# Four chained layers on eight images: fewer projections in layer 1, symmetric halves in layer 3, folded norms, and GpSimd shares

## The chip, the cores and the metric

The kernel runs on one core of a Trainium2 chip. The metric is the time of one execution on the device in microseconds (us). The core has five engines that work side by side, each through its own queue in program order: TensorE (PE; the weight loads of its matmuls are shown apart as PEld), VectorE (DVE), ScalarE (ACT), GpSimd (POOL) and SyncE (SP), which here only issues DMAs. They meet through semaphores alone.

## The reference

The input is eight images of 16 x 16 positions with 128 channels, all fp32. Four layers follow each other:

```
L0: theta, phi, g = x@w_theta, maxpool2x2(x@w_phi), maxpool2x2(x@w_g)   (with biases)
    x1 = x + sigma * (softmax(theta phi^T) g @ w_o + b_o)                256 positions against 64 pooled ones
L1: n = groupnorm(x1; 32 groups) * gamma + beta;  q, k, v = n@wq+bq, n@wk+bk, n@wv+bv
    x2 = x1 + softmax(q k^T / sqrt(128)) v @ wo + bo                     one head of 128
L2: n = groupnorm(x2; 16 groups) * scale + bias;  q, k, v = n@w_qkv
    x3 = x2 + concat_8_heads(softmax(q k^T / 4) v) @ w_out + b_out       eight heads of 16
L3: z = DHT2d(x3)  (cas transform over channels and over w);  zn[h,w] = z[-h,-w]
    o1k = relu(.5(z w1a + zn w1b) + b1_0),  o1n = relu(.5(zn w1a + z w1b) + b1_1)   (8 blocks of 16 channels)
    y = (two block matmuls of o1k, o1n);  out = x3 + DHT2d(softshrink(y, 0.01)) / (16*128)
```

The position reversed in h and w is the same image read backwards, modulo 16 in both directions.

## The kernel before

Everything is unrolled and everything stays in SBUF after the first loads. A layout with channels on the partitions (128 x 256) and one with positions on the partitions (two tiles of 128 positions x 128 channels) alternate. PSUM is used as eight banks of 512 fp32; each matmul group is given its bank by hand (the `b` argument) and waits, where the order of the queue doesn't ensure it, for the semaphore that frees the bank (the `*marks`, through `freed`).

One image passes through these steps. Layer 0: `proj0`, `pool0` (max pooling), `theta`, `pg_out`, `s0` (scores), `nmax0_out`, `exp0`, `p0t` (transposition of the probabilities), `p0c`, `gwm`/`gw` (the values), `o0` (with a column of ones that gives the sums), `inv0_out`, `x1_out` (positions on partitions, divides by the sums and adds `xin`, the input loaded a second time in that layout). Then `x1t`/`xc` transpose to channels on partitions, and the group norm follows: `moments`, `mean`, `mean_square` on DVE, `gm1` on PE (mean over the group), `variance`, `variance_eps`, `inverse_deviation` on POOL (a power of -0.5), `group_scale`, `group_shift`, `normalised`. Layer 1: `qk1` (two projections), `q1`, `k1`, `v1m`/`v1`, `s1`, `nmax1_out`, `exp1`, `p1t`, `p1c`, `o1`, `inv1_out`, `x2_out`; `x1b_out` and `x2b_out` on POOL add the bias of the layer to the residual. `x2t`/`xc` and the same norm lead to layer 2: `qk2`, `qkE`/`qkO`, `v2m`/`va`, `sm` (scores for the maximum, heads in two sets g = 0, 1, four heads at a time in row groups of the array), `nmax2_out`, `nt`, `nc_out`, `spread` (a DMA that writes the negated maxima as a row beside q), `st` (scores transposed, with the maximum in them), `exp2`, `pv`, `oc`, `ot`, `oinv_out`, `on_out`, `ont`, `onc`, `o2`, `x3_out`. Layer 3: `zm`, `zc`, `wrap` (POOL copies row 0 to row 16, so that the reversed read is a plain negative stride), `am` (two accumulated matmuls over 17 x 17 = 289 columns, the second reading `zE` backwards), `o1k_out`, `o1n_out`, `ym`, `yh`, `yn`, `v3`, `s3_out`, `om`, `xo`, `store`.

The eight images are interleaved by an order that is written out for each queue (L319 to L325 for POOL, L630 to L681 for PE, L816 to L837 for ACT, L1021 to L1061 for DVE, L264 to L266 for SP). `keep_clock(n, b)` puts n matmuls on zeros into the PE queue; nobody reads them. The first `sm` in PE's order is that of image 0 (L641); after the last `pv`, that of image 7 (L679), only the ends of images 5 to 7 are left.

The input comes in by `load_x` and `load_tokens` for each image (128 KB each) and four tables of weights.

```python
both = bank[b][:, 0:EXT].rearrange("p (h w) -> p h w", h=HE)
mm(both, fold1[:, 0, :], zE(i), start=True, stop=False)
mm(both, fold1[:, 1, :], zE(i)[:, ::-1, ::-1], start=False, stop=True).then_inc(s["a"], 1)
```

Of the kernel before, what the change touches and what calls it, by code (L numbers as in the profile page):

```python
# [23 lines left out]
EXT = HE * WE  # L24
# [5 lines left out]
COLUMNS = ("b_phi_g", "b_theta", "sigma", "L1_conv_gn_gamma", "L1_conv_gn_beta", "L1_conv_bq", "L1_conv_bk",  # L30
# [15 lines left out]
def table(t):  # L46
# [23 lines left out]
    at("cas_w")[:] = np.kron(np.eye(tile_h), cas(W))  # L70
# [43 lines left out]
def build(nc, x, xT, weights, out):  # L114

    x_tok = x.rearrange("b (u h) w c -> b (h w) u c", u=TILES)
    out_tok = out.rearrange("b (u h) w c -> b (h w) u c", u=TILES)

    with ExitStack() as ctx:
# [14 lines left out]
        def col(name):  # L134
# [5 lines left out]
        wvo, bo1_wide = sb("wvo", [P, C]), sb("bo1_wide", [P, C])  # L140
        w2qs = sb("w2qs", [P, C])
# [7 lines left out]
        bq_s, c_t0, c_t1, c_low, c_high, half = (  # L149
            sb(n, [P, 1]) for n in ("bq_s", "c_t0", "c_t1", "c_low", "c_high", "half"))  # L150
# [4 lines left out]
        xin = ring("xin", [P, TILES, C], IMAGES)  # L155
# [62 lines left out]
        def wide(tile):  # L218
            return tile.unsqueeze(1).to_broadcast((P, TILES, C))
# [5 lines left out]
        def _(sp):  # L225
            def load_x(i):
                sp.dma_start(x0T(i), xT[i]).then_inc(s[f"x0T{i}"], 16)

            def load_tokens(i):
                sp.dma_start(xin(i), x_tok[i]).then_inc(s[f"xin{i}"], 16)  # L230
# [34 lines left out]
            spread(3, 1); store(1); spread(4, 0); spread(4, 1); spread(5, 0); store(2); spread(6, 0); spread(5, 1)
            spread(6, 1); spread(7, 0); store(3); spread(7, 1); store(4); store(5); store(6); store(7)  # L266
# [3 lines left out]
        def _(pool):  # L270
            gp = nc.gpsimd

            def fill():
# [39 lines left out]
            def wrap(i):  # L313
# [763 lines left out]
```

## Time and profile before

| what | value |
| --- | --- |
| runs of the kernel before | 174.29, 173.12, 173.66 us; median 173.66 us |
| profiled execution: time | 173.37 us |
| profiled execution: span from the first to the last instruction | 171.5 us |
| PE busy in the span | 96% |
| granted clock of TensorE, mean over the span | 0.999 |

The profiled execution took 1.9 us outside its span. A busy PE is not a PE at its peak: matmuls are pipelined, and one that is shown with 400 ns may be followed by the next after half of that. What a matmul costs is the distance from start to start, which the chain of work shows.

### The profile page before, as it was taken

The numbers are of one execution on the slowest core, as the hardware profiler recorded it, in microseconds if no ns is written. First come the engines' busy times: TensorE is split into PE (matmuls) and PEld (weight loads), VectorE is DVE, ScalarE is ACT, GpSimd is POOL, SyncE is SP. The second block draws the span as 40 slices with busy tenths as digits, with TensorE's granted clock in tenths as the row PEclk, the third lists the DMA queues.
The fourth block names the chain that finished last, engine by engine and source line by source line (L and its number), as shares of the span: only waits on it lengthen the run. The fifth ranks groups of instructions, "written<-read, shape, count | busy, mean of one in ns | idle before, by whom it ended". The sixth has DMA issues, their size and how long they took to land.

```text
span 171.5 us, 3846 instructions
## 1 busy us (share of the span) xinstructions
PE 164.8 (96%) x1473; PEld 124.0 (72%) x1473; DVE 109.1 (64%) x293; ACT 109.4 (64%) x251; POOL 27.5 (16%) x56
## 2 busy tenths in 40 slices
PE   7999979999999999999999999999999999999992
PEld 4687869887767777686888776677857675657881
DVE  1368899899977886837967634979175566123032
ACT  0467568686565788385467877374867856874660
POOL 8011714232122111120011210000011000000100
PEclk9999999999999999999999999999999999999999
DMA  5992000000000000000001001000010000200003
GB/s 139 303 325 108 4 2 2 0 4 0 2 2 4 0 4 6 0 6 0 0 4 34 2 0 36 0 6 2 2 36 2 4 2 2 64 3 6 0 0 92
DMA packets 6353, 5.17 MB, mean 30 GB/s; under 512 B 576, under 2 KB 5952, under 8 KB 6336
## 3 DMA queue, kind: packets, MB, share of 16 engines
q1 hardware_dynamic: 6336, 4.93, 9.5%
q8 instruction: 12, 0.20, 0.4%
q14 instruction: 5, 0.04, 0.1%
HBM read 3.75 MB, written 1.05 MB: 28 GB/s over the span
## 4 chain that ended last, share of the span: by engine, by line
PE 83%; DMA 4%; DVE 4%; ACT 3%; SPq 2%; issue 1%; POOL 0%; DVEq 0%; POOLq 0%
PE psum L537 10%; PE psum L517 9%; PE psum L548 9%; PE psum L445 4%; PE psum L465 4%; DMA x0T<-in_xT 3%; PE psum L599 3%; PE psum L425 2%; PE psum L559 2%; PE psum L455 2%; ACT pT L779 2%; PE psum L618 2%; PE psum L600 2%; PE psum L610 2%; PE psum L575 2%; PE psum L589 2%
## 5 line engine op out<-in xcount | busy, mean ns | idle before, releaser
L984 DVE TENSOR_REDUCE nmax<-psum 128x4 f32<-128x1024 f32 x32 | 38.1, 1216 | 9.1 <-PE psum L517 8.9
L779 ACT ACTIVATE pT<-psum 128x1024 f32<-128x1024 f32 x32 | 32.1, 1022 | 9.3 <-PE psum L537 9.3
L537 PE MATMUL psum<-qk 17*128 17x256 f32 (+1 forms) x256 | 18.3, 400 | 0.2 <-DMA qk<-stage_all 0.2
L517 PE MATMUL psum<-qk 16*128 16x256 f32 (+1 forms) x256 | 18.3, 400 | 0.0
L548 PE MATMUL psum<-pT,vaug_all 128*32 128x256 f32 x256 | 16.5, 384 | 0.0
L517 PEld LDWEIGHTS psum<-qk 16*128 16x128 f32 (+1 forms) x256 | 11.6, 184 | 4.9 <-issue 1.8
L537 PEld LDWEIGHTS psum<-qk 17*128 17x128 f32 (+1 forms) x256 | 11.6, 184 | 4.1 <-ACT oT L784 0.8
L311 POOL TENSOR_TENSOR rstd<-vare,half 128x1 f32<-128x1 f32 x16 | 8.9, 564 | 31.9 <-DVE vare L936 31.8
L548 PEld LDWEIGHTS psum<-pT,vaug_all 128*32 128x32 f32 x256 | 7.1, 109 | 6.0 <-issue 2.3
L316 POOL COPY zE<-zE 128x17 f32<-128x17 f32 x8 | 1.6, 200 | 52.6 <-ACT zE L792 52.6
L784 ACT COPY oT<-psum 128x256 f32<-128x256 f32 x16 | 6.0, 373 | 5.9 <-PE psum L548 5.8
L304 POOL TENSOR_TENSOR x2b<-x,tab 128x256 f32<-128x256 f32 x8 | 5.8, 727 | 24.5 <-DVE x L974 24.5
L298 POOL TENSOR_TENSOR x1b<-x,bo_wide 128x256 f32<-128x256 f32 x8 | 5.8, 730 | 22.4 <-DVE x L906 22.4
L339 PE MATMUL psum<-busy 128*128 128x256 bf16 x43 | 8.2, 338 | 1.1 <-POOL busy L274 1.1
L1011 DVE SCALAR_TENSOR_TENSOR yneg<-psum,c_high,yhigh 128x256 f32<-128x256 f32 x8 | 3.8, 479 | 7.8 <-ACT yhigh L810 7.8
L990 DVE RECIPROCAL oinv<-psum 128x16 f32<-128x16 f32 x8 | 2.0, 254 | 10.4 <-PE psum L559 10.4
L465 PE MATMUL psum<-v_all,p1T 128*128 128x129 f32 x64 | 8.6, 277 | 0.0
L445 PE MATMUL psum<-k1T,q1T 128*128 128x256 f32 x32 | 8.6, 393 | 0.0
L742 ACT ACTIVATE p<-psum,nmax 128x256 f32<-128x256 f32 x16 | 6.7, 469 | 2.9 <-DVE nmax L962 2.7
L465 PEld LDWEIGHTS psum<-v_all,p1T 128*128 128x128 f32 x64 | 7.9, 191 | 0.7 <-issue 0.5
L752 ACT COPY xT_sb<-psum 128x256 f32<-128x256 f32 x16 | 6.0, 373 | 2.7 <-PE psum L474 1.5
L1018 DVE TENSOR_TENSOR x<-psum,x 128x256 f32<-128x256 f32 x8 | 3.4, 423 | 6.6 <-PE psum L626 6.5
(137 smaller groups left out, 360.1 us busy)
## 6 DMA issues: line engine op xcount, KB each, us to landing
x0T<-in_xT SPq DMA_DIRECT2D x8, 128.0 KB, 4.9
xin<-in_x SPq DMA_DIRECT2D x8, 128.0 KB, 5.0
out<-x SPq DMA_DIRECT2D x8, 128.0 KB, 2.0
tab<-in_weights SPq DMA_DIRECT2D x1, 580.0 KB, 5.3
qk<-stage_all SPq DMA_DIRECT2D x32, 4.0 KB
tab<-in_weights SPq DMA_DIRECT2D x1, 448.0 KB, 5.4
tab<-in_weights SPq DMA_DIRECT2D x1, 384.0 KB, 5.7
tab<-in_weights SPq DMA_DIRECT2D x1, 200.0 KB, 2.5
```

Source lines behind the costliest of these rows:

```text
L311: gp.tensor_tensor(rstd[k](i), vare[k](i), half[:, :], ALU.pow).then_inc(s[f"rstd{layer}"], 1)
L339: mm(bank[b][:, 0:256], busy[:, 0:P], busy[:, :], start=True, stop=True)
L445: last = mm(bank[b][:, u * TOK:(u + 1) * TOK], q1T(i)[:, u * P:(u + 1) * P], k1T(i), start=True, stop=True)
L465: last = mm(bank[b][:, u * (C + 1):(u + 1) * (C + 1)], p1T(i)[:, m, u * P:(u + 1) * P], v1_all[:, i % SLOTS, m, :], start=(m == 0), stop=( ...
L517: last = mm(bank[(b0, b1)[j // 2] + j % 2][:, u * TOK:(u + 1) * TOK], at[:, u, 0, :], at[:, :, 1, :], start=True, stop=True)
L537: last = mm(bank[(b0, b1)[j // 2] + j % 2][:, m * TOK:(m + 1) * TOK], at[:, m, 1, :], at[:, :, 0, :], start=True, stop=True)
L548: last = mm(bank[b][32 * j:32 * j + 32, 0:TOK], vaug_all[:, i % SLOTS, m, QUADS * g + j, :], pT[g](i)[:, j, m, :], start=(m == 0), stop=(m ...
L742: last = go(p1(i)[:, u, :], bank[home["s1", i]][:, u * TOK:(u + 1) * TOK], ACT.Exp, bias=nmax1(i)[:, u:u + 1])
L752: copy(xT_sb[layer - 1](i), bank[home[f"x{layer}t", i]][:, 0:TOK]).then_inc(s[f"xT{layer}"], 1)
L779: go(pT[g](i)[:, 2 * k:2 * k + 2].rearrange("p j m t -> p j (m t)"), pair(home["st", g, i][k]), ACT.Exp).then_inc(s["exp" + "EO"[g]], 1)
L784: copy(oT[g](i), bank[home["pv", g, i]][:, 0:TOK]).then_inc(s["oT" + "EO"[g]], 1)
L984: v.tensor_reduce(nmax2[g](i)[:, :, 2 * k:2 * k + 2], pair(home["sm", g, i][k]).rearrange("p j (u m) -> p u j m", u=TILES), AX.X, ALU.max, ...
```

## The change

Layer 1. The score matrix (n wq + bq)(n wk + bk)^T is written as n (wq wk^T) n^T plus a term for each key position; terms that are the same for all keys of a query fall out of the softmax, but the exponential's bias has to carry the rest. `qk1` is now one projection with a product of weights made once (`w1qk`), `k1` is gone, `s1` takes the normalised image itself as the other operand. A further column of `v1m` gives `e1`, and `score_shift` (POOL) makes the bias `nb1` of `exp1` from it and `nmax1`. The gammas and betas of both norms are folded into weights and bias columns at the start (`fold_biases`, `bias_wide`, `fold_values`, `fold_biases2`, `fold_out2`, `scaled2`, `values_folded`, `bias_sums`, `bias_sums2`, `out2_folded`); `group_scale` and `group_shift` go, and `normalised` subtracts the mean and multiplies by `rstd`.

Residual by channel. `o0` and `o1` give their outputs with channels on the partitions, so `x1` and `x2` are made in that layout: `x1t`, `xc`, `xin` and its loads, `x1b_out` are gone. The sums of the softmax come out of `exp0` and `exp1` (`accum_out`), and the probabilities are divided by them before they are transposed (`p0_scaled`, `p1_scaled`, POOL). `x2t` now transposes `x2b` for the residual of layer 2 alone (`xr`).

Layer 3. Because the reversal maps the 16 x 16 positions onto themselves, POOL makes the sum and the difference of z and its reversal over half the rows (`z_sum`, `z_difference`: 9 x 16 = 144 columns), `am` is one matmul on each, and their sum and difference (`odd_out`, `a_out`) give both halves; `om` undoes the order of the second half by a second block of `cas_w`.

Also moved from DVE to POOL: `pg_out` and `mean_square`. All orders and banks are written anew; the fillers are 28 instead of 43.

```diff
-    (("mean1", P), ("w1_q", C), ("w1_k", C), ("w1_vT", C), ("w1_o", C), ("bv_wide", C), ("bo_wide", C)),
-    (("mean2", P), ("w2_q", C), ("w2_k", C), ("w2_v", C), ("b_out_wide", C), ("w2_o", C)),
-    (("mlp", 6 * P), ("cas_c", C), ("cas_w", P), ("cas_we", P // W * WE)),
+    (("mean1", P), ("w1_q", C), ("w1_k", C), ("w1_v", C), ("w1_qT", C), ("w1_kT", C), ("w1_vT", C), ("w1_o", C),),
+    (("mean2", P), ("w2_q", C), ("w2_k", C), ("w2_v", C), ("w2_o", C)),
+    (("mlp", 6 * P), ("cas_c", C), ("cas_w", 2 * P), ("cas_we", P // W * WE)),
...
-            def load_tokens(i):
-                sp.dma_start(xin(i), x_tok[i]).then_inc(s[f"xin{i}"], 16)
...
+            def z_sum(i, *marks):
+                after(marks)
+                pool.wait_ge(s["zE"], i + 1)
+                gp.tensor_tensor(zsum(i), zE(i)[:, 0:HALF, 0:W], zE(i)[:, H:H - HALF:-1, W:0:-1], ALU.add
+                                 ).then_inc(s["zsum"], 1)
...
+            def pg_out(i, *marks):
+                after(marks)
+                pool.wait_ge(s["pooled"], i + 1)
+                gp.tensor_scalar(pg(i), pooled(i).unsqueeze(1).to_broadcast((P, 2, POOLED)), col("b_phi_g"), None, ALU.add
+                                ).then_inc(s["pg"], 1)
+
+            def mean_square(i, layer, *marks):
+                after(marks)
+                pool.wait_ge(s[f"mv{layer}"], i + 1)
+                m = mv[layer - 1](i)
+                gp.tensor_scalar(m[:, 1:2], m[:, 0:1], m[:, 0:1], m[:, 1:2], ALU.mult, ALU.add).then_inc(s[f"ms{layer}"], 1)
...
+            def p1_scaled(i, *marks):
+                after(marks)
+                pool.wait_ge(s["inv1"], i + 1)
+                for u in range(TILES):
+                    last = gp.tensor_scalar(p1n(i)[:, u, :], p1(i)[:, u, :], inv1(i)[:, u:u + 1], None, ALU.mult)
+                last.then_inc(s["p1n"], 1)
+
+            def score_shift(i, *marks):
+
+                after(marks)
+                pool.wait_ge(s["nmax1"], i + 1)
+                pool.wait_ge(s["v1"], i + 1)
+                for u in range(TILES):
+                    e = e1(i)[:, u:u + 1]
+                    last = gp.tensor_scalar(nb1(i)[:, u:u + 1], nmax1(i)[:, u:u + 1], e, e, ALU.subtract, ALU.add)
+                last.then_inc(s["nb1"], 1)
...
+            pg_out(0); pg_out(1); bias_wide(); p0_scaled(0); scaled2(0); pg_out(2); scaled2(1); scaled2(2)
+            mean_square(0, 1); p0_scaled(1); pg_out(3); mlp_sums(); inverse_deviation(0, 1); p0_scaled(2); pg_out(4)
...
+            def fold_biases(b, *marks):
...
+                for n, name in enumerate(("w1_q", "w1_k", "w1_v")):
+                    last = mm(bank[b][:, n:n + 1], w(name), col("L1_conv_gn_beta"), start=True, stop=True)
...
+                mm(bank[b][:, C:C + 1], w("w1_o"), bqkv[:, 2:3], start=True, stop=True)
+                mm(bank[b][:, 2 * C:3 * C], w("w1_qT"), w("w1_kT"), start=True, stop=True)
+                mm(bank[b][:, 3 * C:3 * C + 1], w("w1_qT"), bqkv[:, 1:2], start=True, stop=True)
+                mm(bank[b][:, 3 * C + 1:3 * C + 2], w("w1_kT"), bqkv[:, 0:1], start=True, stop=True)
+                mm(bank[b][:, 3 * C + 2:3 * C + 3], bq_wide[:, :], bqkv[:, 1:2], start=True, stop=True
+                   ).then_inc(s["fold_vo"], 1)
...
-                mm(bank[b][:, 0:TOK], w("w1_q"), xn[0](i), start=True, stop=True)
-                mm(bank[b][:, TOK:2 * TOK], w("w1_k"), xn[0](i), start=True, stop=True).then_inc(s["qk1"], 1)
...
+                mm(bank[b][:, 0:TOK], w1qk[:, :], xn[0](i), start=True, stop=True).then_inc(s["qk1"], 1)
...
-                for u in range(TILES):
-                    for m in range(TILES):
-                        last = mm(bank[b][:, u * (C + 1):(u + 1) * (C + 1)], p1T(i)[:, m, u * P:(u + 1) * P],
-                                  v1_all[:, i % SLOTS, m, :], start=(m == 0), stop=(m == TILES - 1))
+                for m in range(TILES):
+                    last = mm(bank[b][:, 0:TOK], v1_all[:, i % SLOTS, m, :], p1T(i)[:, m, :],
+                              start=(m == 0), stop=(m == TILES - 1))
...
-                both = bank[b][:, 0:EXT].rearrange("p (h w) -> p h w", h=HE)
-                mm(both, fold1[:, 0, :], zE(i), start=True, stop=False)
-                mm(both, fold1[:, 1, :], zE(i)[:, ::-1, ::-1], start=False, stop=True).then_inc(s["a"], 1)
+                pe.wait_ge(s["zsum"], i + 1)
+                mm(bank[b][:, 0:HALF * W], fold1[:, 0, :], zsum(i).rearrange("p h w -> p (h w)"), start=True, stop=True)
+                pe.wait_ge(s["zdif"], i + 1)
+                mm(bank[b][:, HALF * W:2 * HALF * W], fold1[:, 1, :], zdif(i).rearrange("p h w -> p (h w)"),
+                   start=True, stop=True).then_inc(s["a"], 1)
...
+                for u in range(TILES):
+                    last = mm(bank[b][:, u * C:(u + 1) * C], w("cas_w")[:, u * P:(u + 1) * P], s3(i)[:, u, :],
+                              start=True, stop=True)
...
+            keep_clock(9, 7); proj0(0, 0); keep_clock(3, 7); proj0(1, 1); keep_clock(4, 7); gwm(0, 0, ("theta", 1))
+            s0(0, 2); fold_biases(1, ("theta", 2)); gwm(1, 3); s0(1, 4); proj0(2, 0, ("gw", 1))
...
+                copy(v1_all[:, i % SLOTS, :, 0:C], both[:, :, 1:1 + C])
+                go(e1(i), both[:, :, 0], ACT.Identity, bias=e_bias[:, :], scale=float(C) ** -0.5).then_inc(s["v1"], 1)
...
+                    last = go(p1(i)[:, u, :], bank[home["s1", i]][:, u * TOK:(u + 1) * TOK], ACT.Exp,
+                              bias=nb1(i)[:, u:u + 1], accum_out=sum1(i)[:, u:u + 1])
...
+                copy(odd(i), bank[home["am", i]][:, HALF * W:2 * HALF * W]).then_inc(s["odd"], 1)
...
+                v.tensor_tensor(x1(i), bank[home["o0", i]][:, 0:TOK], x0T(i), ALU.add).then_inc(s["x1"], 1)
...
+                v.scalar_tensor_tensor(out=x2(i), in0=bank[home["o1", i]][:, 0:TOK], scalar=bo1[:, :], in1=x1(i),
+                                       op0=ALU.add, op1=ALU.add).then_inc(s["x2"], 1)
...
+                v.tensor_tensor(a2(i)[:, 0:HALF * W], even, odd(i), ALU.add)
+                v.tensor_tensor(a2(i)[:, HALF * W:2 * HALF * W], even, odd(i), ALU.subtract).then_inc(s["aneg"], 1)
```

## Rows read from the trace of the kernel before

**Rows 1.** The page, part 1: busy time, share of the span, instructions.
```profile
PE 164.8 (96%) x1473; PEld 124.0 (72%) x1473; DVE 109.1 (64%) x293; ACT 109.4 (64%) x251; POOL 27.5 (16%) x56
```

**Rows 2.** The page, part 4: the chain that ended last, by engine.
```profile
PE 83%; DMA 4%; DVE 4%; ACT 3%; SPq 2%; issue 1%; POOL 0%; DVEq 0%; POOLq 0%
```

**Rows 3.** Windows: length, busy of PE, PEld, DVE, ACT, POOL; PEclk, DMA share, GB/s.
```profile
8.90:40.09 31.19, 30.04 (x199) 25.81 (x199) 26.84 (x101) 22.04 (x67) 10.68 (x16) 1.00 0.18 57
40.09:154.70 114.61, 113.93 (x1168) 82.49 (x1168) 75.44 (x176) 77.36 (x161) 12.68 (x24) 1.00 0.03 8
154.70:167.30 12.60, 12.46 (x78) 10.54 (x76) 3.31 (x8) 7.64 (x19) 0.60 (x3) 1.00 0.01 2
```

**Rows 4.** The chain, 60 to 100 us: start, length on it, engine, line.
```profile
68.51 1.08 PE psum L517 x16
69.58 0.37 PE psum L474 x2
...
74.78 0.43 PE psum L425 x2
...
76.08 0.22 PE psum L410 x2
...
80.99 0.49 PE psum L600 x2
...
93.08 0.12 PE psum L483 x2
```

**Rows 5.** The timeline, first microseconds: start, length, engine, operation.
```profile
1.10 2.53 PE L339 MATMUL psum<-busy 128*128 128x256 bf16 x11 [1.10 <-POOL busy L274]
```

**Rows 6.** The chain, 0 to 40.1 us.
```profile
22.04 0.66 PE psum L455 x4
...
29.23 0.98 PE psum L339 x9
...
40.09 1.08 PE psum L517 x16
```

**Rows 7.** Groups of POOL: busy, mean ns of one, idle before.
```profile
L311 POOL TENSOR_TENSOR rstd<-vare,half 128x1 f32<-128x1 f32 x16 | 8.9, 564 | 31.9 <-DVE vare L936 31.8
L304 POOL TENSOR_TENSOR x2b<-x,tab 128x256 f32<-128x256 f32 x8 | 5.8, 727 | 24.5 <-DVE x L974 24.5
...
L316 POOL COPY zE<-zE 128x17 f32<-128x17 f32 x8 | 1.6, 200 | 52.6 <-ACT zE L792 52.6
...
L289 POOL TENSOR_TENSOR mlp_a<-mlp_half 128x384 f32<-128x384 f32 x1 | 1.0, 997 | 1.5 <-DVE mlp_half L858 1.5
...
L276 POOL MEMSET thetaT_all<- 128x768 f32 x1 | 0.7, 739 | 0.0
```

**Rows 8.** The timeline at 25.9 us.
```profile
25.92 0.76 DVE L924 SCALAR_TENSOR_TENSOR mv<-mv 128x1 f32<-128x1 f32 x1
25.94 0.73 POOL L304 TENSOR_TENSOR x2b<-x,tab 128x256 f32<-128x256 f32 x1 [3.28 <-DVE x L974]
```

**Rows 9.** The line of `mean_square`: ns min/median/max, first and last start.
```profile
L924 DVE SCALAR_TENSOR_TENSOR mv<-mv x16: 202/219/761, 13.7 to 128.9; 128x1 f32<-128x1 f32 x16
```

**Rows 10.** Groups of DVE and ACT.
```profile
L947 DVE SCALAR_TENSOR_TENSOR gsh<-psum,gsc,tab 128x1 f32<-128x1 f32 x16 | 3.5, 217 | 0.4
...
L1002 DVE TENSOR_TENSOR x<-psum,x2b 128x256 f32<-128x256 f32 x8 | 3.3, 420 | 3.6 <-PE psum L575 3.6
...
L752 ACT COPY xT_sb<-psum 128x256 f32<-128x256 f32 x16 | 6.0, 373 | 2.7 <-PE psum L474 1.5 <-PE psum L410 1.0
...
L720 ACT COPY p0T<-psum 128x128 f32<-128x128 f32 x8 | 2.1, 268 | 1.9 <-PE psum L394 1.8
...
L689 ACT ACTIVATE bq_s<-tab 128x1 f32<-128x1 f32 x1 | 0.2, 203 | 0.8 <-DMA tab<-in_weights 0.8
```

**Rows 11.** The chain, 150 us to the end.
```profile
153.65 1.07 PE psum L548 x16
...
168.25 0.42 DVE x L1018
```

More of the change, by code:

```diff
@@ L271, in _, with after @@
             gp = nc.gpsimd
+            def after(marks):
+                for name, value in marks:
+                    pool.wait_ge(s[name], value)
             def fill():
@@ new lines, in _ @@
+            p1_scaled(5); inverse_deviation(4, 2); mean_square(7, 1); score_shift(6); x2b_out(5); mean_square(5, 2)
+            p1_scaled(6); wrap(0); z_difference(0); z_sum(0); inverse_deviation(5, 2); inverse_deviation(7, 1)
+            x2b_out(6); mean_square(6, 2); wrap(1); z_difference(1); z_sum(1); score_shift(7); inverse_deviation(6, 2)
+            p1_scaled(7); wrap(2); z_difference(2); z_sum(2); x2b_out(7); mean_square(7, 2); inverse_deviation(7, 2)
+            wrap(3); z_difference(3); z_sum(3); wrap(4); z_sum(4); z_difference(4); wrap(5); z_difference(5); z_sum(5)
@@ L327, in _ @@
+            wrap(6); z_difference(6); z_sum(6); wrap(7); z_difference(7); z_sum(7)
         @block.tensor
@@ L636, in _ @@
-            o1(0, 5); v1m(1, 2, ("theta", 6)); qk1(1, 7); gwm(4, 1, ("fold1_rd", 1), ("c_rd", 1))
-            gwm(5, 2, ("v1", 2)); x2t(0, 5); s0(4, 3); gm1(2, 7, ("k1", 2)); s1(1, 5, ("xT2", 1))
-            x1t(3, 1, ("gw", 5)); s0(5, 2, ("gw", 6)); p0t(4, 3); keep_clock(9, 4); qk1(2, 7); gm2(0, 3, ("p0T", 5))
-            p1t(1, 2, ("p0", 6)); gm1(3, 1); o0(4, 5); s1(2, 7); o1(1, 4); qk2(0, 0, ("theta", 7)); v1m(2, 3)
-            x2t(1, 7, ("p1", 3)); p1t(2, 4); p0t(5, 1, ("gsh1", 4)); qk1(3, 7, ("xT2", 2)); o0(5, 1); x1t(4, 2)
@@ L641, in _ @@
-            v1m(3, 0, ("qkO", 1)); gm2(1, 5); s0(6, 4); s1(3, 7); sm(0, 0, 0, 2, ("v1", 4), ("x1", 6))
-            x1t(5, 4, ("p0", 7)); o1(2, 6); p1t(3, 7); sm(0, 1, 0, 4, ("nmaxE", 1), ("xT1", 6)); v2m(0, 7, ("p1T", 4))
-            nt(0, 0, 2); o1(3, 3); p0t(6, 2, ("stageE", 1)); gwm(6, 7); x2t(2, 2, ("p0T", 7)); keep_clock(1, 6)
-            o0(6, 7); nt(0, 1, 2, ("xT2", 3)); st(0, 0, 4, 0); gm2(2, 2, ("stageO", 1)); qk2(1, 6)
-            v2m(1, 4, ("expE", 1)); gm1(4, 5); gm1(5, 0, ("expE", 2)); pv(0, 0, 4, ("vaug", 2)); x2t(3, 3)
@@ L646, in _ @@
-            keep_clock(5, 1); qk2(2, 6, ("qkO", 2)); sm(1, 0, 4, 2, ("gsh1", 5), ("oTE", 1)); v2m(2, 0, ("gsh1", 6))
-            v1m(4, 6, ("qkO", 3)); qk1(4, 1); qk1(5, 6, ("v1", 5)); sm(1, 1, 2, 4, ("nmaxE", 4))
-            nt(1, 0, 7, ("x1", 7)); x1t(6, 1, ("k1", 5)); v1m(5, 6, ("k1", 6)); s0(7, 7, ("stageE", 2))
-            st(0, 1, 2, 0, ("nmaxO", 3), ("xT1", 7)); gm2(3, 6, ("v1", 6)); gwm(7, 7, ("p0", 8)); nt(1, 1, 4)
-            s1(4, 5); s1(5, 7, ("gw", 8)); gm1(6, 4, ("stageO", 2)); p0t(7, 2); pv(0, 1, 3); p1t(4, 5)
@@ new lines, in _ @@
+            s0(0, 2); fold_biases(1, ("theta", 2)); gwm(1, 3); s0(1, 4); proj0(2, 0, ("gw", 1))
+            fold_values(2, ("p0", 1)); p0t(0, 3, ("gw", 2)); fold_biases2(1); proj0(3, 5); o0(0, 3)
+            gwm(2, 0, ("theta", 3)); proj0(4, 4); s0(2, 2, ("vo_rd", 1)); fold_out2(0, ("gw", 3)); proj0(5, 1)
+            proj0(6, 3, ("x1", 1)); proj0(7, 6); keep_clock(4, 7); gm1(0, 2, ("p0", 3)); keep_clock(3, 7); p0t(1, 0)
+            keep_clock(3, 7); gwm(3, 5, ("theta", 4)); o0(1, 0); s0(3, 7); fold_mlp(4, 5, ("theta", 5)); qk1(0, 2)
@@ new lines, in _ @@
+            o0(5, 7); o1(1, 2); gm1(3, 1, ("p1", 3)); qk2(0, 0); v2m(0, 2, ("x2", 2)); p1t(2, 6, ("x1", 5))
+            s0(6, 3, ("gw", 8)); s0(7, 2, ("vaug", 1)); gm2(1, 4); o1(2, 6); gm1(4, 0, ("qkO", 1)); qk1(3, 1)
+            v1m(3, 3, ("p0", 7)); x2t(0, 6, ("x2", 3)); x2t(1, 2, ("p0", 8)); s1(3, 1); qk2(1, 6, ("x2r", 1))
+            sm(0, 1, 2, 4, ("x2r", 2)); x2t(2, 0, ("xn1", 5)); gm2(2, 7); v1m(4, 1, ("p1", 4))
+            gm1(5, 2, ("nmaxO", 1)); qk1(4, 6, ("qkO", 2)); p0t(6, 0, ("x2r", 3)); v2m(1, 3); nt(0, 1, 1, ("v1", 5))
@@ L841, in _, with after @@
             v = nc.vector
+            def after(marks):
+                for name, value in marks:
+                    dve.wait_ge(s[name], value)
             def scale_w0():
```

681 lines of the change are left out of this document (358 added, 323 removed).

## The prediction

> **What bounds the kernel now.** I read the page first, for the shares: PE is busy for 96% of the span, its weight loads for 72%, VectorE and ScalarE for 64% each, GpSimd for 16% [rows 1]. Busy time of PE can mislead, so the chain of waits comes next: PE holds 83% of it, and no other engine over 4% [rows 2]. Third, the distances on that chain, which are what a matmul really costs. A projection of 256 fp32 columns takes 0.43 us (two passes), two transposes of 128 columns 0.22, one half of `am` with its 289 columns 0.49, a group mean of 2 columns 0.12, eight score matmuls in row groups 1.08 [rows 4]. The first full-array group behind such a row-grouped one costs more: two transposes 0.37 instead of 0.22 [rows 4].
>
> With these prices I add up the PE order. It holds 144.5 us of work and 43 fillers. A filler takes 0.98 / 9 = 0.109 us at full clock [rows 6], 4.6 us in all. The span is divided by two marks in the order: the first `sm` starts at 40.09 [rows 6], the last `pv` ends at 153.65 + 1.07 = 154.7 [rows 11].
> - Ramp, to 40.1: 27.0 us of work and 3.6 of fillers. The rest is loading and waits for layer 0 and 1 of the first images.
> - Middle, 114.6 us [rows 3]: 105.5 us of work, 0.75 of fillers, and 33 changes from row or column groups back to the full array at 0.37 - 0.22 = 0.15, 5.0. That leaves 3.4 us, so PE is the bound here.
> - Tail, 154.7 to 171.5: 16.8 us, of which 12.0 are work. PE is busy for 12.46 of the first 12.60 us [rows 3]; then come the last additions [rows 11] and the store.
>
> A rule speaks against reading the middle so. The Trainium skill (Perfetto Trace Analysis, Identifying the Most-Contended Engine) says to judge TensorE's headroom by the busy time of its weight loads and not by that of its matmuls. By 82.5 of 114.6 us [rows 3] a quarter of the middle would be free, and less matmul work would then gain less than its length; that is the second rival below.
>
> **The change on PE.** Removed, each times eight images: one of the two projections of `qk1`, 0.43, is 3.44 us; `x1t`, 0.22, is 1.76; `am` goes from 2 x 289 to 2 x 144 columns, so from 0.98 to 0.98 x 144 / 289 = 0.49, is 3.92 [rows 4]. Sum 9.1. `o0`, `o1`, `v1m`, `s1` and `om` keep their columns within 1% and are costed at nothing; `x2t` stays. Added once: ten matmuls of one column (three in `fold_biases`, four in `fold_values`, two in `fold_biases2`, one in `fold_out2`) at 0.12 each [rows 4], 1.2; the product of the two weight matrices takes the place of a bias matmul of the same 128 columns. Net 7.9 us less work, 136.5. The fillers go from 43 to 28, but a filler lies where PE would wait, so its removal need not gain. Changes from groups to the full array: 32 instead of 34, nothing.
>
> Now the same three stretches by the new order. *Ramp:* more lies ahead of the first `sm` (two `gwm`, one `s0`, an `o1`, a `qk2`, a `v2m`, a `gm1`, the folds: 4.3) and less (five `x1t` 1.1, four projections 1.7), +1.5; fillers -0.9. So 40.7, if the waits stay. *Middle:* less by three `x1t` (0.7), four projections (1.7), five `am` (2.5), what went ahead (3.1), three `v3` and `om` that go to the tail (2.6), and more by one `ont` and `o2` (0.7): -9.9. I leave the time of its 0.75 us of fillers standing as waits: 104.7. *Tail:* work +2.6 - 0.7 - 1.5 = +0.5, and a longer path for image 7, below: 17.5 instead of 16.8.
>
> **The other engines.** VectorE loses 16 each of `mean_square`, `group_scale` and `group_shift` at about 0.22 us [rows 9, 10], and `pg_out`, 8 at under 0.42: 12 us; it gains `a_out`, 16 operations of 144 columns between 0.22 and 0.42 [rows 10], at 0.30 (between 1 and 256 columns) 4.8, and 11 small folds at 0.22, 2.4: about 104 us. ScalarE loses `xc` (6.0) and `k1` (8 at 0.37 or more, 3.0); it gains `xr` 8 x 0.37, `odd_out` 8 x 0.28 (268 ns for 128 columns, 373 for 256), `e1` 8 x 0.20 [rows 10], and 32 sums by `accum_out`. The trace has none of these: from 0 to a small operation of 203 ns each [rows 10], 0 to 6.5 us; I take 3, the middle, since nothing says more. About 110 us, no change. Neither bounds a span of 162 us; both hide beside PE.
>
> GpSimd is the disputed part. It goes from 56 instructions to about 135. Operations of two tensors cost 727 ns for 256 columns and 997 for 384, so 190 ns fixed and 2.1 ns per column; a fill of 768 columns takes 739 and a copy of 17 takes 200, so 0.72 ns per column; but the power takes 564 for one column [rows 7]. For a `tensor_scalar` with column operands, the trace has nothing: the low price is 190 ns + 0.72 per column, the high one 560 + 2.1. Ahead of the first `sm` stand 8 `pg_out` (128), 12 halves of `p0_scaled` (64), 6 of `p1_scaled` (256), 7 `mean_square`, 6 of `score_shift`, 3 `scaled2` and `bias_wide` (128), with 6 powers, 2 `x2b`, 2 `mlp_sums`: 17 us low, 38 high, in the 31 us from 8.9 to there [rows 3]. I take the low end, a copy being the nearest row in kind. The Trainium skill (GPSIMD Engine Reference, Elementwise — side-by-side cycle accounting) puts two-input operations at about twice VectorE's time and one-input ones near its rate; the first agrees with 727 against 420 ns, the second no row here shows.
>
> **Latencies.** On an image's way through layers 0 and 1 there go `x1t` and `xc` with their hops (0.8 us, and as much at `x2t`), twice scale and shift (0.5 each), and `k1` (0.4): 3.0. There come `p0_scaled` (2 x 0.24 to 0.69), `score_shift` (2 x 0.19 to 0.56) and `p1_scaled` (2 x 0.37 to 1.10), with hops 2.0 to 5.0. So -1.0 to +2.0, near nothing. `qk1` of image 0 now also waits for `fold_values`, which wait for table 1, a bias sum on VectorE and `bias_wide` on GpSimd, behind which `p0_scaled`(0) and all of GpSimd stand; and `inverse_deviation`(0, 1) stands behind `mlp_sums`, which wait for table 3. Eight input loads of 128 KB fewer bring the tables earlier. I count +1 us for image 0 and get it back from image 1 on, whose norm chain is shorter; the ramp's waits stay. The `am` of each image now waits for `wrap`, `z_difference` and `z_sum` (2 x 0.49 by the two-tensor price [rows 7]), then `odd_out` and `a_out`; `z_sum`(7) stands last on GpSimd, and `wrap`(3) and `wrap`(4) stand behind `inverse_deviation`(7, 2). In the middle other images' work hides this. In the tail image 7 gets 2 x 0.49 + 0.35 + 0.60 - 0.49 and hops, +1.6. PE's 12.5 us of work cover some of it: 0 to 1.6, I take 0.7 for the tail. SP's `spread`(4, 0) stands behind `store`(0) and `store`(1), which wait for `xo`; `st`(4, 0) comes far enough behind `om`(1) to hide that.
>
> **A port.** `mean_square` of 1 column takes 219 ns in the median but 761 at worst, and 760 at 25.92, when GpSimd adds from 25.94 to 26.67 [rows 8, 9]. The Trainium skill (SBUF — State Buffer, Who interferes with whom) has such a pair wait for each other when the VectorE operation has two SBUF inputs and GpSimd reads SBUF; the trace agrees. The operation goes, but GpSimd reads more than before, and 16 `variance_eps` have the same form: 0 to 16 x 0.54 = 8.7 us on VectorE, at most 2 us of it on the ramp's chain. I take nothing, and keep the 2 us for the range.
>
> **The sum.** 40.7 + 104.7 + 17.5 = 162.9, with the 1.9 us outside the span 164.8 against the execution's 173.4; 8.6 less. The median of the runs is 0.3 above that execution. I say 165.0.
>
> **Rivals.**
> 1. *GpSimd becomes the ramp's bound (slower).* If its column-operand instructions cost like the power, 38 us stand in a window of 31, and its queue is in order, so each norm waits behind the scalings of other images. The ramp grows by the overflow, 7, by the first image's longer way, 2, and by the port's 2; once they pass 8.6 us together the gain is eaten. 164.8 + 11 = 175.8. For it: the 564 ns for one column. Against: every other row of GpSimd, and 16% load now.
> 2. *The work wasn't the bound.* If the middle hangs on the chains score, maximum, DMA, exponential, `pv`, its 9.9 us shrink by the share that the weight loads leave free, 28%, and image 7 pays its full 1.6 instead of 0.7: 164.8 + 2.8 + 0.9 = 168.5. For it: the rule above. Against: 3.4 us unexplained of 114.6.
> 3. *No change.* The rewritten order costs about a us per image that this trace can't show: 164.8 + 8 = 172.8.
> A clock risk belongs to the forecast's range: PE begins at 2.53 / 11 = 0.23 us for a filler of 256 columns [rows 5] against 0.109 later, the lower of its two clocks, 1.2 against 2.4 GHz. With 16 fillers instead of 23 ahead of layer 0 it may rise later; 1 to 2 us of work at half speed cost 1 to 2 us.
>
> **How the numbers follow.** Forecast, with its clock and port terms, 162 to 168: 0.70. Rival 2 0.15, rival 3 0.07, rival 1 0.06; faster than 162, 0.02. The range 161.5 to 169.5 leaves out about 0.15. What a measurement here can tell from no change is about 1%, 171.9 to 175.4: faster 0.87, same 0.07, slower 0.06.
>
> **What the profile would show.** On the chain `qk1` is one pair of 0.43, `am` two pairs of 0.25; the first `sm` near 40.7, the last `pv` ending near 145.4, the tail 17.5; GpSimd busy for about 50 us with `p1_scaled` near 0.37 each; full clock by 8 us. Wrong would be: column-operand operations on GpSimd over 0.5 us for one column, PE gaps over 6 us in the middle, ScalarE over 115 us.

## The result, and the profile after

The changed kernel takes 172.49 us (median of 15 runs), the kernel before 173.09 (15 runs). The ratio of the two is 0.9945, 95% interval 0.9926 to 0.9963. So it is 0.55% faster, where 165.0 was forecast and 161.5 to 169.5 allowed. Four of its 15 runs took 177.5 to 177.6 us; the ratio leaves them out, and e9 and e12 below ask why they are so slow. The profiled execution took 171.77 us with a span of 170.0.

The page, part 1, and the first line of part 4:

```profile
PE 157.4 (93%) x1446; PEld 118.7 (70%) x1446; DVE 98.8 (58%) x248; ACT 110.9 (65%) x282; POOL 66.3 (39%) x137
...
PE 68%; POOL 13%; DVE 7%; ACT 5%; issue 3%; DMA 2%; SPq 0%; DVEq 0%; ACTq 0%
```

PE is busy for 7.4 us less than before, VectorE 10 us less, ScalarE 1.5 us more [rows 1]. GpSimd has gone from 27.5 to 66.3 us, where the prediction had about 50, and it holds 13% of the chain, where it had 0% [rows 2].

The same three stretches as in [rows 3], by the windows (length, then busy us of PE, PEld, DVE, ACT, POOL). The first `sm` begins at 45.6, the last `pv` ends at 152.9:

```profile
9.00:45.60 36.60, 33.12 (x216) 27.77 (x215) 23.65 (x97) 23.15 (x90) 27.54 (x54) 1.00 0.05 18
45.60:152.90 107.30, 102.95 (x1098) 73.52 (x1097) 66.92 (x130) 75.80 (x162) 30.95 (x61) 1.00 0.02 5
152.90:167.00 14.10, 14.08 (x106) 12.44 (x102) 6.26 (x18) 8.91 (x24) 3.30 (x9) 1.00 0.13 37
```

| stretch | before | forecast | after | second-op form (e1) | all cheap forms, `mean_square` on VectorE, early fillers (e11) |
| --- | --- | --- | --- | --- | --- |
| ramp, to the first `sm` | 40.1 | 40.7 | 45.6 | 43.7 | 42.1 |
| middle | 114.6 | 104.7 | 107.3 | 105.6 | 105.6 |
| tail | 16.8 | 17.5 | 17.1 | 17.0 | 17.0 |
| span | 171.5 | 162.9 | 170.0 | 166.3 | 164.7 |

The middle gained 7.3 of 9.9 us, and the ramp lost 5.5. In the ramp GpSimd is busy for 27.5 of 36.6 us and PE has 3.5 us without a matmul, against 1.1 before [rows 3]. What it does there, as groups over the whole span (busy, mean ns of one, idle before):

```profile
L352 POOL TENSOR_SCALAR p1n<-p,inv 128x256 f32<-128x256 f32 x16 | 14.8, 934 | 4.9 <-DVE inv L1083 4.9
...
L345 POOL TENSOR_SCALAR p0n<-p,inv 128x64 f32<-128x64 f32 x16 | 7.2, 473 | 1.4 <-DVE inv L1031 1.4
L362 POOL TENSOR_SCALAR nb<-nmax,e 128x1 f32<-128x1 f32 x16 | 6.0, 399 | 18.5 <-DVE nmax L1077 18.5
L339 POOL TENSOR_SCALAR mv<-mv 128x1 f32<-128x1 f32 x16 | 5.4, 336 | 5.6 <-DVE mv L1048 5.5
L332 POOL TENSOR_SCALAR pg<-pooled,tab 128x128 f32<-128x128 f32 x8 | 4.9, 617 | 3.2 <-DVE pooled L1019 3.2
L295 POOL TENSOR_TENSOR x2b<-x,b_out 128x256 f32<-128x256 f32 x8 | 4.9, 612 | 7.0 <-DVE x L1089 6.9
...
L326 POOL TENSOR_SCALAR w2n<-tab 128x128 f32<-128x128 f32 x3 | 1.1, 373 | 0.0
```

`p1_scaled` costs 934 ns for 256 columns; the low price said 374, the high one 1100. Two operations of one image take 1.86 us in a row. The line that helps most is the last: `scaled2` (tile `w2n`) does two operations on 128 columns in 373 ns, `pg_out` one operation on 128 in 617.

The chain of waits shows the queue (start, length, engine, line; "issue" is time in which no wait is seen):

```profile
14.88 0.34 POOL mv L339
15.21 1.13 POOL p0n L345 x2
16.34 0.46 POOL pg L332
16.81 0.09 issue
16.89 0.64 POOL mlp_a L285
17.53 0.05 issue
17.58 0.72 POOL mlp_b L287
18.30 0.53 POOL rstd L303
18.82 0.89 POOL p0n L345 x2
19.72 1.79 POOL pg L332 x3
21.50 0.33 POOL mv L339
```

From 14.9 to 21.8 us the path that sets the end runs through GpSimd alone. The norm of image 1 is at `mean_square` (21.50) behind three `pg_out` for images 4 to 6, which nobody needs yet. Over the ramp from 9 us on, GpSimd holds 17.1 us of the chain, where it held 0.6 before.

### The profile page after: what moved, and what is told of

It is laid out like the page before. It is cut to its first block, busy times and chain, and to the rows that moved or that the text cites. A ratio compares the mean times of both kernels' runs of the same rounds, so it can differ in the third digit from the quotient of the medians.

```text
span 170.0 us, 3873 instructions
## 1 busy us (share of the span) xinstructions
PE 157.4 (93%) x1446; PEld 118.7 (70%) x1446; DVE 98.8 (58%) x248; ACT 110.9 (65%) x282; POOL 66.3 (39%) x137
## 4 chain that ended last, share of the span: by engine, by line
PE 68%; POOL 13%; DVE 7%; ACT 5%; issue 3%; DMA 2%; SPq 0%; DVEq 0%; ACTq 0%
PE psum L621 9%; PE psum L632 9%; PE psum L601 7%; POOL p1n L352 4%; DVE nmax L1098 4%; ACT pT L876 3%; PE psum L529 3%; PE psum L548 3%; POOL p0n L345 3%; PE psum L702 2%; PE psum L673 2%; PE psum L659 2%; PE psum L711 2%; PE psum L694 2%; PE psum L643 2%
## 5 line engine op out<-in xcount | busy, mean ns | idle before, releaser
L621 PE MATMUL psum<-qk 32*128 32x256 f32 (+1 forms) x256 | 18.2, 398 | 0.0
L601 PE MATMUL psum<-qk 32*128 32x256 f32 (+1 forms) x256 | 17.9, 393 | 0.0
L352 POOL TENSOR_SCALAR p1n<-p,inv 128x256 f32<-128x256 f32 x16 | 14.8, 934 | 4.9 <-DVE inv L1083 4.9
L621 PEld LDWEIGHTS psum<-qk 32*128 32x128 f32 (+1 forms) x256 | 11.6, 184 | 3.9 <-issue 1.2
L601 PEld LDWEIGHTS psum<-qk 32*128 32x128 f32 (+1 forms) x256 | 12.0, 184 | 3.3 <-issue 1.2
L362 POOL TENSOR_SCALAR nb<-nmax,e 128x1 f32<-128x1 f32 x16 | 6.0, 399 | 18.5 <-DVE nmax L1077 18.5
L830 ACT ACTIVATE p<-psum,nb 128x256 f32<-128x256 f32 x16 | 7.4, 470 | 4.7 <-POOL nb L362 4.7
L1069 DVE TENSOR_SCALAR xn<-x,psum,rstd 128x256 f32<-128x256 f32 x16 | 7.2, 451 | 4.7 <-POOL rstd L303 3.9
L529 PE MATMUL psum<-xn,t1T 128*128 128x256 f32 x32 | 8.8, 397 | 0.0
L849 ACT ACTIVATE qk<-psum,q_bias 128x512 f32<-128x512 f32 x8 | 5.5, 688 | 4.9 <-PE psum L578 4.9
L548 PE MATMUL psum<-p1T,v_all 128*128 128x256 f32 x32 | 8.6, 392 | 0.0
L345 POOL TENSOR_SCALAR p0n<-p,inv 128x64 f32<-128x64 f32 x16 | 7.2, 473 | 1.4 <-DVE inv L1031 1.4
```

The costliest lines, as they stand in the source:

```text
L345: last = gp.tensor_scalar(p0n(i)[:, u, :], p0(i)[:, u, :], inv0(i)[:, u:u + 1], None, ALU.mult)
L352: last = gp.tensor_scalar(p1n(i)[:, u, :], p1(i)[:, u, :], inv1(i)[:, u:u + 1], None, ALU.mult)
L529: last = mm(bank[b][:, u * TOK:(u + 1) * TOK], t1T(i)[:, u * P:(u + 1) * P], xn[0](i), start=True, stop=True)
L548: last = mm(bank[b][:, 0:TOK], v1_all[:, i % SLOTS, m, :], p1T(i)[:, m, :], start=(m == 0), stop=(m == TILES - 1))
L601: last = mm(bank[(b0, b1)[j // 2] + j % 2][:, u * TOK:(u + 1) * TOK], at[:, u, 0, :], at[:, :, 1, :], start=True, stop=True)
L621: last = mm(bank[(b0, b1)[j // 2] + j % 2][:, m * TOK:(m + 1) * TOK], at[:, m, 1, :], at[:, :, 0, :], start=True, stop=True)
```

## The experiments

"First `sm`" and "end of the last `pv`" are read from the instructions of those lines, as in the table. The 51.9 in the expectations of e1 and e2 is the changed kernel's second group of `sm` (the first that lies on the chain); its first begins at 45.6.

Each run is timed beside the kernel before, and "ratio" is always to that. Where a gain is split into stretches, the two profiled executions are compared.

**e1: the same GpSimd work in another form.** Three lines changed:

```diff
-  gp.tensor_scalar(pg(i), ..., col("b_phi_g"), None, ALU.add)
+  gp.tensor_scalar(pg(i), ..., col("b_phi_g"), 0.0, ALU.add, ALU.add)
-  gp.tensor_scalar(p0n(i)[:, u, :], p0(i)[:, u, :], inv0(i)[:, u:u + 1], None, ALU.mult)
+  gp.tensor_scalar(p0n(i)[:, u, :], p0(i)[:, u, :], inv0(i)[:, u:u + 1], 1.0, ALU.mult, ALU.mult)
   (p1_scaled likewise)
```

> The three GpSimd steps pg_out, p0_scaled and p1_scaled keep their place and gain a second operation without effect (times 1.0, plus 0.0), the form of scaled2, which took 372 ns for 128 columns where pg_out took 617. If the price of GpSimd's single-operation form sets the ramp: p1_scaled falls from 934 ns to some 500 to 650, the first sm comes 3 to 5 us before 51.9, and the time falls to 167 to 169. If the form isn't what costs (the column operand is, or the port): durations and time as they are, 172 to 173. If latencies of hops between engines set the ramp and not GpSimd's load: durations fall but the time moves by under 1 us.

Measured: 168.1 us, ratio to before 0.9714 (0.9697 to 0.9730). The groups, and the windows of the ramp and the middle:

```profile
L352 POOL TENSOR_SCALAR p1n<-p,inv 128x256 f32<-128x256 f32 x16 | 7.5, 482 | 5.5 <-DVE inv L1083 5.5
...
L332 POOL TENSOR_SCALAR pg<-pooled,tab 128x128 f32<-128x128 f32 x8 | 5.9, 736 | 2.9 <-DVE pooled L1019 2.9
...
L345 POOL TENSOR_SCALAR p0n<-p,inv 128x64 f32<-128x64 f32 x16 | 5.2, 336 | 1.3 <-DVE inv L1031 1.3
```
```profile
9.00:43.70 34.70, 32.45 (x217) 27.82 (x215) 23.36 (x97) 23.03 (x90) 24.25 (x54) 1.00 0.05 20
43.70:149.30 105.60, 102.47 (x1098) 73.47 (x1098) 66.68 (x130) 75.79 (x162) 26.04 (x61) 1.00 0.02 5
```

Orders and waits are the same; only 8 us of GpSimd's busy time are gone (66.3 to 58.3), and 4.4 us of time with them. Between the profiled executions it is 3.7 us: 1.9 in the ramp, 1.7 in the middle, 0.1 in the tail. On the ramp's chain GpSimd's part falls from 17.1 to 9.6 us. So GpSimd's price, not the structure, took at least that. `pg_out` got dearer (736 ns), so it isn't a second operation as such that makes the form cheap.

**e2 to e4: the work on VectorE instead.** `p0_scaled` and `p1_scaled` directly behind `inv0_out` and `inv1_out`; then also `pg_out` behind `pool0`; then also `mean_square` and `score_shift`.

```diff
-  gp.tensor_scalar(p1n(i)[:, u, :], p1(i)[:, u, :], inv1(i)[:, u:u + 1], None, ALU.mult)
+  v.tensor_scalar(p1n(i)[:, u, :], p1(i)[:, u, :], inv1(i)[:, u:u + 1], None, ALU.mult)
...
-  ... inv1_out(0); variance(2, 1) ...
+  ... inv1_out(0); p1_scaled(0); variance(2, 1) ...
```

> p0_scaled and p1_scaled run on VectorE right behind inv0_out and inv1_out; GpSimd loses 22 us of its 66. GpSimd-bound ramp: first sm 5 to 8 us earlier than 51.9, time 165 to 168. If VectorE, now with some 10 us more in the ramp, takes its place: first sm 1 to 3 us earlier, 170 to 172. If the removed PE work wasn't on the path at all: the ramp shortens and the middle grows by as much, 171 to 173.

> As the run before, and pg_out on VectorE behind pool0 (4.9 us less on GpSimd, 2.2 more on VectorE). GpSimd-bound ramp: another 1 to 2 us, 164 to 167. VectorE-bound ramp: the same or slower than the run before.

> As the run before, and mean_square and score_shift on VectorE too, so that GpSimd keeps the power, x2b, the folds and layer 3. If what is left of GpSimd's share still delays the norms: 163 to 166, first sm near 42. If VectorE's queue is now the ramp's bound (score_shift waits there for v1 from ScalarE, with everything behind it waiting too): 166 to 170.

Measured: e2 169.05 us (ratio 0.9767, 0.9750 to 0.9785), e3 169.97 (0.9817, 0.9799 to 0.9836), e4 0.9957 (0.9926 to 0.9989), its runs scattered from 171.2 to 178.7 us. The ramps of e2 and e3, to the same time:

```profile
9.00:44.00 35.00, 33.01 (x222) 28.59 (x221) 28.29 (x115) 23.84 (x91) 17.37 (x36) 1.00 0.05 17
```
```profile
9.00:44.00 35.00, 31.64 (x218) 27.72 (x217) 28.57 (x118) 23.46 (x90) 12.55 (x28) 1.00 0.06 20
```

In e2 GpSimd's ramp load falls to 17.4 us and VectorE's rises to 28.3 of 35: the first `sm` comes at 44.1, 1.5 us earlier than after the change. The gain of 3.4 us is less than e1's with all work left on GpSimd, but not clearly so: in e2's profiled execution the clock rose later and its third projection starts 0.7 us later (10.12 against 9.42). In e3, whose third projection starts at 10.18, GpSimd has 12.6 us and it gets slower, first `sm` 45.4. VectorE has become the queue: it holds 12.6 us of the ramp's chain in e2 and 12.3 in e3, against 4.1 after the change, and GpSimd 1.5 and 1.9. In e4 VectorE holds 23% of the whole chain, against 14% in e2 and e3, and the time lies above both expected ranges. What holds it up there, the wait for `v1` inside `score_shift` or the load, wasn't taken apart.

**e5: the saved work put back on PE.** `qk1` and both matmuls of `am` issued twice in the changed kernel:

```diff
+  mm(bank[b][:, 0:TOK], w1qk[:, :], xn[0](i), start=True, stop=True)
   mm(bank[b][:, 0:TOK], w1qk[:, :], xn[0](i), start=True, stop=True).then_inc(s["qk1"], 1)
   (both matmuls of am likewise)
```

> The changed kernel with its saving on TensorE taken away and all else kept: qk1's projection and both matmuls of am are issued twice (3.4 and 3.9 us of work). If PE binds the middle and the tail but GpSimd the ramp: the four projections of the ramp (1.7) cost nothing, the rest most of its length, +4 to +6, so 176 to 178. If the saving was never on the path: 172 to 174. If it was wholly on it: 179.5.

Measured: 177.37 us, 4.9 more than the changed kernel, for 7.4 us of work. The windows of its middle and tail:

```profile
51.80:162.60 110.80, 106.92 (x1126) 77.56 (x1126) 66.91 (x130) 75.98 (x162) 30.92 (x61) 1.00 0.02 5
162.60:180.90 18.30, 15.52 (x114) 13.80 (x114) 6.69 (x19) 9.09 (x24) 3.30 (x9) 0.99 0.15 44
```

The middle takes 110.8 us against 107.3, for 4.2 us of work put back there (four projections, five `am`), and the tail 18.3 against 17.1, for 1.5 (three `am`): 4.7 of 5.6 us, 84%. What the other four projections cost in the ramp this profile can't tell, since its clock rose late (below); the 4.9 us leave nearly nothing for them. So most of the saving on PE was on the path outside the ramp, and it is what carries the change: with it taken away the changed kernel is 2.4% slower than the one before (ratio 1.0236, 1.0201 to 1.0272).

**e6: the kernel before, with a load on GpSimd in front of the norms of layer 1.**

```diff
+  for at, width in ((0, 64), (64, 64), (128, 128), (256, 256), (512, 256)):
+      last = gp.tensor_scalar(spare[:, at:at + width], tab[:, first:first + width], col("sigma"), None, ALU.mult)
...
   pool.wait_ge(s[f"vare{layer}"], i + 1)
```

> The kernel before, whose GpSimd multiplies, ahead of each power of layer 1, columns of a table into a tile that nobody reads: two of 64, one of 128, two of 256 columns, the single-operation form (3.4 us for each image, 27 in all). If GpSimd's load in front of the norms alone costs the changed kernel its gain: the first sm comes 4 to 10 us later than 40.0 and the time is 177 to 183. If load on GpSimd is harmless there: 173 to 174.

Measured: 189.07 us, ratio 1.0905 (1.0851 to 1.0958), more than the 177 to 183 expected. The groups, then a window of the ramp:

```profile
L317 POOL TENSOR_SCALAR spare<-tab 128x256 f32<-128x256 f32 x16 | 14.6, 925 | 0.0
```
```profile
34.00:42.00 8.00, 6.75 (x23) 5.85 (x24) 4.57 (x19) 2.41 (x6) 4.04 (x8) 0.57 0.00 1
```

The multiplication costs 925 ns here too, in a kernel with none of the other edits, so the price belongs to the form. The first `sm` comes at 48.3 instead of 40.0. PE waited 3.2 us for VectorE's `xn` up to 35.25, and the granted clock is 0.57 from 34 to 42 us, the lower of the two levels for most of it; from 66 to 72 it is 0.50. So the 16 us are load and clock together and no measure of the load alone.

**e7 and e8: what is left of GpSimd's share.** On top of e1, once `pg_out` as multiply by 1.0, add the column; once `mean_square` back on VectorE.

```diff
-  gp.tensor_scalar(pg(i), ..., col("b_phi_g"), 0.0, ALU.add, ALU.add)
+  gp.tensor_scalar(pg(i), ..., 1.0, col("b_phi_g"), ALU.mult, ALU.add)
```

> As the first run (168.1), but pg_out multiplies by 1.0 and adds the column, instead of adding the column and 0.0 (736 ns). If multiply first is what makes a GpSimd operation cheap: some 370 to 400 ns for 128 columns, 3 us less load, 166 to 168. If the broadcast input is what costs: 700 ns and 168.

> As the first run (168.1), and mean_square on VectorE behind mean, as before the change: 16 x 0.34 us and two hops of about 0.1 us leave the norm's way. If GpSimd's queue in front of the norms still sets the ramp: 166.5 to 167.8. If VectorE's queue matters as much: 168 to 169.

Measured: e7 166.87 us (ratio 0.9630, 0.9595 to 0.9664); e8 166.9 and 167.1 in two runs (0.9644, 0.9600 to 0.9687) and 172.6 and 172.7 in the other two, of the kind that e9 asks about. The group of e7:

```profile
L332 POOL TENSOR_SCALAR pg<-pooled,tab 128x128 f32<-128x128 f32 x8 | 2.9, 369 | 3.5 <-DVE pooled L1019 3.5
```

The same output costs 617 ns as one addition, 736 as two, 369 as multiply and add. Each edit takes a further 1.1 to 1.3 us; the first `sm` comes at 42.4 and 42.5.

**e9 and e12: the fillers.** The changed kernel with the 11 and 8 early fillers of the kernel before, and the kernel before with the 9 and 3 of the changed one.

```diff
-  keep_clock(9, 7); proj0(0, 0); keep_clock(3, 7); proj0(1, 1); keep_clock(4, 7);
+  keep_clock(11, 7); proj0(0, 0); keep_clock(8, 7); proj0(1, 1); keep_clock(4, 7);
```

> The changed kernel with 11 and 8 fillers around the first proj0, as in the kernel before, instead of 9 and 3; all else kept. In the profile of the fifth run the projections of images 2 to 7 took 0.85 us for 256 columns until some 20 us, in the changed kernel's own 0.43 from 7 us on. If too little work before 7 us leaves the rise of the clock to chance: every run near 172.5 and none some 5 us above. If the fillers have nothing to do with it: some runs above as before. If they delay layer 0: up to 0.5 us more.

> The kernel before with 9 and 3 fillers around the first proj0, as the change has them. If the early fillers decide the clock's rise: some of the runs 3 to 6 us above 173. If not: all at 173, or up to 0.5 us less.

Measured: e9 171.8 us, ratio 0.9917 (0.9885 to 0.9950), five runs from 171.7 to 172.0 and none at 177. e12 175.7 us, four runs from 175.5 to 176.1, ratio 1.0146 (1.0112 to 1.0180): all of them 2.5 to 3.0 us above, where some by 3 to 6 had been expected. PE's timeline of the kernel before at its third projection, of e12 at the same one, and of e5's profiled execution at image 4:

```profile
8.90 0.70 PE L369 MATMUL psum<-x0T,tab 128*128 128x256 f32 x2
```
```profile
9.72 1.06 PE L369 MATMUL psum<-x0T,tab 128*128 128x256 f32 x2
```
```profile
17.89 1.06 PE L460 MATMUL psum<-x0T,tab 128*128 128x256 f32 x2
```

A projection spans 1.06 us at the lower clock (its two passes start 0.43 us apart) and 0.59 to 0.70 at the upper. In e12 the upper one comes after the third projection, near 13 us; in e5's execution, which took 182.73 us against some 177.3 for its others, only at about 20 us. So fewer fillers put the rise off: in the kernel before by about the same in all four runs, to judge by their times, in the changed kernel by more in some executions than in others. Counted over the changed kernel and its variants, 15 of 56 runs with 16 early fillers lie 4 to 7 us above the rest of their kernel (e1 to e5, e7, e8 and e10 with them), and none of the 10 with 23 (e9, e11). At the same rate none in 10 would come by luck in about one case of 20, so this is likely and not certain. That the changed kernel's runs at 177.6 are such executions is inferred from this count and from e5's profile; none of them was profiled. e4's profiled execution, 176.84 us, has the same late rise, so its ramp isn't compared here.

**e10 and e11: together.** e7 with `mean_square` on VectorE, and the same with the early fillers.

> The seventh run (cheap forms of pg_out, p0_scaled and p1_scaled, 166.9) and the eighth (mean_square on VectorE) together. If both shorten the same queue of GpSimd and it still sets the ramp: 165 to 166. If the ramp is by now set by TensorE and the chain itself (first sm near 41, forecast 40.7): 166 to 167.

> The tenth run with 11 and 8 fillers: its time within 0.5 us, and no run some 5 us above.

Measured: e10 167.09 us with two of six runs at 172.3 and 172.4 (ratio 0.9637, 0.9604 to 0.9669), e11 166.75 us, five runs from 166.5 to 166.9 (0.9628, 0.9596 to 0.9659). The page of e11:

```profile
PE 156.4 (95%) x1453; PEld 119.2 (72%) x1453; DVE 102.6 (62%) x264; ACT 110.8 (67%) x282; POOL 50.1 (30%) x121
```

It is 3.7% faster than the kernel before and 3.3% faster than the changed one. The two edits of e7 and e8 don't add up: with either, the first `sm` comes at 42.4 or 42.5, with both at 42.8 (e10, whose third projection starts 0.7 us late, at 10.11) and with the fillers at 42.1. GpSimd no longer sets the ramp: it holds 1.5 us of the ramp's chain in e11, and PE 17.7.

## Why the prediction was wrong

**The step that failed: GpSimd's price for a `tensor_scalar` with column operands.** The trace of before had none. The prediction bounded it (190 ns + 0.72 per column, 560 + 2.1) and took the low end, "a copy being the nearest row in kind". So it let GpSimd's queue hide beside PE in the ramp and in the middle, and it does in neither. Measured: 446 ns for 64 columns and 930 for 256 (medians), so 2.5 ns per column and 285 fixed; the slope lies at the high end. All 16 of `p1_scaled` lie between 922 and 948 ns, so chance waits for the port are hardly in it. `mean_square` and `score_shift`, two operations on one column, take 336 and 399 against 190. GpSimd's load in the ramp was 27.5 us after the ninth microsecond alone, against 17 low and 38 high in all. The two-tensor addition's 2.1 ns per column would have come nearer, but only by luck: multiply and multiply calculates too, and costs 0.76. The result lies between forecast and first rival, whose mechanism (GpSimd's in-order queue holds up the norms) is what the chain shows; only its size was smaller, 5 us in the ramp and not 11. Of the 7.1 us by which the span missed its 162.9, the ramp has 4.9 and the middle 2.6, and the tail gives back 0.4. That rival had been given 0.06, and no case stood for "the mechanism at half its price", the likeliest of all between two bounds so far apart.

**"The ramp's waits stay", 40.7.** Wrong by 4.9 us. e1 takes 1.9 of them away by price alone, e7 and e8 1.3 and 1.2 more but not together; 1.4 are left in e11, and their cause stays open. The latencies between bounds of -1.0 and +2.0 were taken as nothing; with measured prices the three new steps cost 0.9 + 0.8 + 1.9 us and hops of 0.3 to 0.4, about 4.0 against the 3.0 that go, so near +1. The "+1 us for image 0", which was to come back from image 1 on, stood on no row.

**The middle, 104.7.** Measured 107.3, and 105.6 once the scalings are cheap, within 0.9 of the sum of distances. Taking GpSimd's scalings as hidden there was wrong by 1.7 us: in the changed kernel PE waited for `p1_scaled` in the middle too, as in the chain at 71.40 (e1's chain has no `p1_scaled` from 60 to 80 us):

```profile
71.23 0.08 DVE inv L1083
71.31 0.09 issue
71.40 1.86 POOL p1n L352 x2
73.27 0.04 issue
73.31 0.66 PE psum L539 x4
```

**The work on PE, -7.9.** Right. The middle's distances add up to within 0.9 us of what was measured in e1, and in e5 3.5 of the 4.2 us put back there are paid for, 83%. With it falls the second rival, though by less than it seems. It had 72% of the middle's saving come back, 7.1 of 9.9 us, and the changed kernel's 7.3 looks like it; but the number is luck, since e1 has 9.0 (91%) with TensorE's work and weight loads as they were. The Trainium skill's rule (Perfetto Trace Analysis, Identifying the Most-Contended Engine) read by its weight loads alone would have had a quarter of the middle free; the distances from start to start came nearer.

**The tail, 17.5.** Measured 17.1, so it grew by 0.3 and not by 0.7.

**The other engines.** VectorE 98.8 against 104, ScalarE 110.9 against 110: near enough to change nothing.

**The port, 0 to 8.7 us, taken as nothing.** Right in size. `variance_eps`, for which it was feared, never took more than 269 ns, against 590 at worst before, and `mean_square`, now on GpSimd, never more than 342. One `p0_scaled` took 751 ns instead of 446, as VectorE's `halves` ran; both in the timeline:

```profile
15.06 0.57 DVE L994 TENSOR_SCALAR mlp_half<-tab 128x768 f32<-128x768 f32 x1
...
15.18 1.16 POOL L345 TENSOR_SCALAR p0n<-p,inv 128x64 f32<-128x64 f32 x2
```

**The clock, 1 to 2 us in the range.** Too small where it strikes: about 5 us in four of 15 runs, if those are late rises. The cause was named (16 fillers instead of 23 ahead of layer 0), the price was read from too short a stretch: in e5's execution all that PE does up to some 20 us runs at the lower clock, the first five projections among it.

## What to carry to other kernels

Work moved to an idle engine must be priced in the very form and length in which it will run there; where the trace has no such row and the bounds lie a factor of two or more apart, a value halfway is a case with a chance of its own, and measuring the one instruction first is cheaper than any argument. An engine at 39% of the span can be the bound of one stretch: ask for its load in the stretch and for what its in-order queue puts ahead of the critical step. And fillers that keep the clock are part of a kernel's time: with fewer, look at the spread of the runs, not only at their median.

## What the runs showed of the hardware

- GpSimd's `tensor_scalar` on fp32 in SBUF depends on its pair of operations: multiply alone 446 ns for 64 and 930 for 256 columns; multiply and multiply 336 and 482, so 0.76 ns per column instead of 2.5. Multiply and add 369 ns for 128 columns, add alone 617, add and add 736. A multiplication by 1.0 that does nothing takes off 25% at 64 columns, 40% at 128 and 48% at 256.
- The Trainium skill (GPSIMD Engine Reference, Engine selection) calls one-input operations on GpSimd "roughly line-rate" beside VectorE. On VectorE (e2) `p1_scaled` takes 350 ns for 256 columns; on GpSimd it takes 482 as multiply and multiply, 1.4 times that, which agrees roughly, and 934 as multiply alone, 2.7 times, which doesn't.
- An addition of a broadcast column as two-tensor operation takes 612 ns for 256 columns, against 727 for two full operands [rows 7].
- TensorE's clock rose from its lower to its upper level at about 7 us in each profile with 23 early fillers. With 16 it rose near 7 us in some profiles, near 9 in others (a pair of `gwm` at 7.6 still takes 0.79 us in e10, against 0.49), near 13 in e12 and near 20 in e4 and e5. In e6, whose PE had waited 3.2 us up to 35.25, the granted clock was 0.57 from 34 to 42 us.
